# A fused attention-like and mixture-of-experts layer on one core: splitting two more products, folding dt into z's, and moving the router one loop pass later

## The reference, cut to what matters

```python
x = x + layernorm(attn(layernorm(x)))      # stage "p" makes q and h, stage "a" the rest
x = x + layernorm(ffn(layernorm(x)))       # stage "f"
# attn (a state-space mixer):
q = rope(x @ W_in[:256].T)                 # only q of qkv is used; it is also the residual
h = rmsnorm(q, norm_pre_w)
z, xBC, dt = split(h @ W_zxbcdt.T)         # 512, 768 and 8 columns
dt = softplus(dt + dt_bias); xBC = silu(conv4(xBC))
y = scan(x_ssm, dt, A, B, C) + D * x_ssm   # by chunks: decays exp(cumsum), a state between chunks
out = rmsnorm(y * silu(z), norm_gated_w) @ W_out.T + q
# ffn: a shared expert of 512 hidden and 16 routed ones of 64, the best 4 (of 2 groups) by token
c = route(sigmoid(x @ router_w.T) + correction_bias)
y = silu(x @ Wg) * (x @ Wu) [* c for the routed] @ Wd
```

## Time and profile before

| what | value |
|---|---|
| three runs | 3399.42, 3401.08, 5217.82 us (median 3401.08) |
| the profiled execution | 3397.91 us, span 3396.1 us |
| TensorE busy | 3259.8 us, 96% of the span, 18624 products |
| VectorE, GpSimd, ScalarE busy | 2450.5, 2159.6, 1830.1 us |
| mean granted TensorE clock | 0.987 of full speed |
| DMA | 210.40 MB, 62 GB/s on average |

### The profile page before, as it was taken

How to read it: one execution, slowest core, us unless ns; L and a number is a source line. 1 busy time by engine, 2 the same in 40 slices (tenths; PEclk the granted TensorE clock), 3 DMA queues, 4 the chain that set the end, 5 groups by cost and what they waited for, 6 DMA issues and landing times. The chain is left out here.

```text
span 3396.1 us, 58363 instructions
## 1 busy us (share of the span) xinstructions
PE 3259.8 (96%) x18624; PEld 2744.5 (81%) x18624; DVE 2450.5 (72%) x4881; ACT 1830.1 (54%) x3247; POOL 2159.6 (64%) x2247
## 2 busy tenths in 40 slices
PE   4799999999999999999999999999999999999997
PEld 3588888888888888888888888888888888888886
DVE  3677777777777777777777777777777777777772
ACT  3455555555555555555555555555555555555552
POOL 1476666776666776666776666766666766666764
PEclk8799999999999999999999999999999999999998
DMA  3022212112212112212122211122211122211121
GB/s 103 31 64 70 70 46 70 56 62 69 69 44 73 58 62 69 69 44 67 57 69 69 69 44 63 62 69 69 69 44 58 61 74 69 69 44 56 62 69 44
DMA packets 126236, 210.40 MB, mean 62 GB/s; under 512 B 18432, under 2 KB 71168, under 8 KB 126208
## 3 DMA queue, kind: packets, MB, share of 16 engines
q1 hardware_dynamic: 126208, 210.06, 18.8%
HBM read 174.87 MB, written 18.35 MB: 57 GB/s over the span
## 5 line engine op out<-in xcount | busy, mean ns | idle before, releaser
L524 POOL TENSOR_TENSOR hidL<-hid,hidH 128x512 fp32r<-128x512 f32 x384 | 492.8, 1283 | 670.3 <-ACT hidH L746 670.3
L951 DVE SCALAR_TENSOR_TENSOR xc<-apb,cw,xc 128x511 f32<-128x511 f32 (+2 forms) x576 | 430.7, 748 | 93.5 <-ACT xc L661 72.5
L519 POOL TENSOR_TENSOR hid<-hid,cb 128x512 f32<-128x512 f32 x256 | 412.7, 1612 | 75.9 <-POOL hidL L524 40.9
L1412 PE MATMUL acc<-WDH,hidH 128*128 128x256 f32 x1536 | 456.5, 297 | 4.4 <-POOLq L526 4.2
L1064 DVE TENSOR_TENSOR hid<-hid,fpb 128x512 f32<-128x512 f32 x384 | 263.6, 687 | 249.6 <-PE fpb L1240 205.2
L1412 PE MATMUL acc<-WDL,hidH 128*128 128x256 f32 x1536 | 433.0, 282 | 0.0
L1412 PE MATMUL acc<-WDH,hidL 128*128 128x256 f32 x1536 | 432.2, 281 | 0.0
L746 ACT CAST hidH<-hid 128x512 fp32r<-128x512 f32 x384 | 236.9, 617 | 333.1 <-POOL hid L519 321.9
L1240 PE MATMUL fpb<-fTh,GH 128*128 128x512 f32 x768 | 335.0, 436 | 6.5 <-ACTq L738 6.5
L1240 PE MATMUL fpb<-fTh,UH 128*128 128x512 f32 x768 | 326.8, 426 | 0.5 <-DVEq L867 0.5
L1412 PEld LDWEIGHTS acc<-WDH,hidH 128*128 128x128 f32 x1536 | 290.4, 189 | 30.0 <-POOLq L526 22.9
(11 more groups left out here) (185 smaller groups left out, 8427.0 us busy)
## 6 DMA issues: line engine op xcount, KB each, us to landing
seg<-acs_row SPq DMA_DIRECT2D x128, 512.0 KB, 5.1
cb<-c_row SPq DMA_DIRECT2D x512, 128.0 KB, 2.9
xsP<-in_x SPq DMA_DIRECT2D x32, 512.0 KB, 6.0
xs<-in_x SPq DMA_DIRECT2D x32, 512.0 KB, 5.3
x<-tmp SPq DMA_DIRECT2D x32, 512.0 KB, 2.9
out<-x SPq DMA_DIRECT2D x32, 512.0 KB, 2.9
ZL_loaded<-in_wzx_t SPq DMA_DIRECT2D x2, 640.0 KB, 5.4
GL_loaded<-in_wg_t SPq DMA_DIRECT2D x2, 512.0 KB, 6.6
```

Source lines behind the costliest of these rows:

```text
L519: G.tensor_tensor(hid[:, j % 2, :], hid[:, j % 2, :], cb[:, r % 2, :], ALU.mult).then_inc(sem["routed_ready"], 1)
L524: own.do(G.tensor_tensor(hidL[:, j % 2, :], hid[:, j % 2, :], hidH[:, j % 2, :].bitcast(fp32), ALU.subtract))
L951: ins = V.scalar_tensor_tensor(xc[:, b, s:], src[:, 0:T - s], cw[:, b, TAPS - 1 - s:TAPS - s], xc[:, b, s:], ALU.mult, ALU.add)
L1412: ins = nc.tensor.matmul(dst, l[:, w, tk], r[:, j, :], start=j == 0 and t % 2 == 0 and n == 0, stop=j == HB - 1 and n == 2, skip_group_che ...
```

## The change

- `WQ` and `WO` are kept as high and low parts (split at the start like the other weights); x's transposes (`xTh`, `xTl`, half a sequence each) and y's (`yTh`, `yTl`) too, and q's and the output's products are three `float32r` ones each.
- dt's eight columns stand behind the first half of z's; z is made in eight products of 264 or 256 columns (`za0`..`zb3`) instead of four of 512, and `project_dt` is gone.
- `exp_seg` takes the token's cumulated sum as the exponent's bias, in eight instructions of 128 columns, and `decay_exponents` is gone; `mask` waits for the DMA itself.
- q is copied by a DMA from `qrot` to `tmp`, which now shares memory with blocks 0 and 1 of `xc` (`xs` with 2 and 3); `mixed_out` adds in place. `norm_mixed` on ScalarE is gone: `add_x` multiplies by the norm's factor and adds x, and the norm's shift, a number per token, is left out of x1 there and added to the final norm's shift (`held`).
- x1 is stored into the output itself by `save_x1`, and GpSimd issues a DMA that adds the final normed result to it in DRAM (`accum_op`); `final_sum` and `store` are gone.
- The router's transposes and logits move from stage a to stage f, that is to the next pass, and the last two `down`s with the final norm to a new stage g, one pass later still. The loop now has 29 passes, after one with p, a and f, and there is one more pass at the end with g alone.
- All five lists are written in another order.

```diff
+            def save_x1(i):
                 sp.wait_ge(sem["x1_ready"], 1)
+                sp.dma_start(out[i].rearrange("(t p) d -> p t d", p=P), tmp).then_inc(sem["x1_stored"], 16)
+                sp.wait_ge(sem["x1_stored"], 16)
+                sp.sem_inc(sem["tmp_free"], 1)
+                sp.sem_inc(sem["x1_in_place"], 1)
+            def keep_q():
+                sp.wait_ge(sem["q_whole"], 1)
+                sp.wait_ge(sem["xc_read"], 1)
+                sp.dma_start(tmp, qrot[:]).then_inc(sem["q_kept"], 16)
...
+            def iteration(i, p, a, f, g):
+                if f: save_x1(i - 1)
+                if a: decay_store(); decay_rows(0); decay_rows(1)
+                if f: combine_store(); combine_rows(0)
+                if p: load_next(i + 1)
                 if f: combine_rows(1)
+                if a: decay_rows(2); decay_rows(3)
+                if f: combine_rows(2)
+                if a: keep_q()
+                if f: combine_rows(3)
+                if a: load_x(i)
+                if f: combine_rows(4); combine_rows(5); combine_rows(6); combine_rows(7)
                 if p: settle_p()
                 if a: settle_a()
...
+                G.tensor_scalar(fnm[:], fmv[:, :, 0], -1.0, 0.0, ALU.mult, ALU.add)
+                own.do(G.tensor_scalar(fve[:], fmv[:, :, 1], 1.0, EPS, ALU.mult, ALU.add))
+                own.do(G.tensor_tensor(frstd[:], fve[:], mhalf[:], ALU.pow))
+                own.do(G.tensor_tensor(fnm[:], fnm[:], frstd[:], ALU.mult))
+                own.do(G.tensor_tensor(fnm[:], fnm[:], held[:], ALU.add))
+                pool.sem_inc(sem["frstd_ready"], 1)
+            def hold_shift():
+                own.do(G.tensor_scalar(held[:], shift[:], 1.0, 0.0, ALU.mult, ALU.add))
+            def add_result(i):
                 pool.wait_ge(sem["normalised"], 1)
+                pool.wait_ge(sem["x1_in_place"], 1)
+                G.dma_start(out[i].rearrange("(t p) d -> p t d", p=P), xn[:], accum_op=ALU.add
+                            ).then_inc(s_stored, 16)
+            def result_stored():
+                pool.wait_ge(s_stored, 16)
+                G.inc_swdge_sem([s_stored], [16], mode="sub")
+                pool.sem_inc(sem["xn_free"], 1)
...
+            def iteration(i, p, a, f, g):
+                if g: norm_out()
+                if f: rest(0)
+                if g: add_result(i - 2)
+                if f: rest(1); rest(2)
                 if a: mask(0)
+                if f: hold_shift()
+                if a: mask(1)
+                if g: result_stored()
+                if a: decayed(0); decayed(1)
+                if f: rest(3); combine(4)
+                if a: gated(0)
...
+                if a: norm_mixed(1); norm_x1(0)
                 if f: combine(10)
                 if a: norm_x1(1)
+                if f: combine(11); rest(10); rest(11)
...
+                for h in range(HS):
+                    ins = A.activation(seg[:, c % 2, h, :], seg[:, c % 2, h, :], ACT.Exp,
+                                       bias=acs[:, 0, c * HS + h:c * HS + h + 1])
...
+            def iteration(p, a, f, g, w=False):
                 for names in freed.values():
                     names.clear()
                 if w: silu_table()
+                if a: conv_first(4); silu_z(0, 0); silu_z(1, 0)
+                if f: f_high(0); f_high(1)
+                if a: conv_first(5); conv_silu(4); silu_z(2, 0); conv_silu(5); exp_table(); softplus()
+                if a: conv_first(0); silu_table(); silu_z(3, 0)
                 if f: gate(0)
+                if a: conv_first(1); conv_silu(0)
+                if f: score_tanh()
+                if a: conv_first(2)
                 if f: round_hidden(0)
+                if a: conv_silu(1)
                 if f: gate(1)
+                if a: silu_z(0, 1); conv_silu(2)
                 if f: gate(2)
+                if g: final_norm()
+                if a: conv_first(3)
+                if f: round_hidden(1)
+                if a: silu_z(1, 1)
+                if f: round_hidden(2)
...
+                if a: evac_y(3); square_y(3)
                 if f: round_hidden(9)
+                if p: square_q(1)
+                if f: gate(10)
+                if p: h_high(0); h_high(1)
+                if f: gate(11)
                 if a: norm_x1(0)
                 if f: round_hidden(10)
+                if a: norm_x1(1)
                 if f: round_hidden(11)
...
+            def x_low(s):
+                dve.wait_ge(sem["xh_ready"], s + 1)
+                free("p", f"xT{s}", V.tensor_tensor(xTl[:], by_half(bank(f"xT{s}")), xTh[:].bitcast(fp32), ALU.subtract))
...
+            def dt_bias_add(c):
+                filled(dve, "DVE", f"za{c}")
+                ins = V.tensor_tensor(dr[:, c, :], bank(f"za{c}")[:, DI // 2:DI // 2 + HS], dtb[:], ALU.add)
+                if c < NT - 1:
+                    ins.then_inc(sem["dt_read"], 1)
+                else:
+                    own.do(ins)
+                    dve.sem_inc(sem["dt_read"], 1)
+                    V.scalar_tensor_tensor(na[:], dr[:], -1.0, dr[:], ALU.mult, ALU.min).then_inc(sem["na_ready"], 1)
...
+                dve.wait_ge(sem["mixed_stats"], s + 1)
                 if s == 0:
                     dve.wait_ge(sem["x_loaded"], 16)
-                own.do(V.tensor_tensor(tmp[:, pair(s), :], tmp[:, pair(s), :], xs[:, pair(s), :], ALU.add))
+                for t in ts:
+                    ins = V.scalar_tensor_tensor(tmp[:, t, :], tmp[:, t, :], rstd[:, t:t + 1], xs[:, t, :],
+                                                 ALU.mult, ALU.add)
+                own.do(ins)
...
+            def iteration(p, a, f, g, w=False):
+                for names in freed.values():
+                    names.clear()
+                if a: dt_bias_add(0); dt_bias_add(1); conv(4)
+                if f: f_low(0)
+                if a: dt_bias_add(2)
+                if f: f_low(1)
+                if a: conv(5)
+                if f: route_logits()
+                if a: dt_bias_add(3)
+                if g: final_moments()
+                if a: dt_finish(); conv(0)
+                if f: up(0)
+                if a: conv(1); conv(2)
+                if f: route_scores()
+                if a: evac_acs()
+                if f: up(1); route_groups(); up(2)
+                if a: conv(3)
+                if f: route_experts(); up(3)
+                if a: times_dt(0); times_dt(1); decay_CB(0)
                 if f: up(4)
+                if a: new_state(0); chunk_y(0)
                 if f: up(5)
+                if a: state_part(1); decay_CB(1)
+                if a: new_state(1); times_dt(2); chunk_y(1)
+                if p: moments_px()
                 if f: up(6)
+                if a: state_part(2); decay_CB(2); y_low(0); new_state(2)
+                if a: chunk_y(2); times_dt(3); decay_CB(3)
+                if p: x_low(0)
+                if a: y_low(1)
                 if f: up(7)
+                if p: rope(0)
+                if a: mixed_out(0)
+                if a: state_part(3)
                 if f: up(8)
+                if a: chunk_y(3); y_low(2)
+                if p: x_low(1)
+                if a: add_x(0)
                 if f: up(9)
+                if a: y_low(3)
+                if p: rope(1); norm_q(0)
                 if a: mixed_out(1)
                 if f: up(10)
+                if p: norm_q(1); h_low(0)
                 if a: add_x(1)
+                if p: h_low(1)
                 if f: up(11)
...
-                    tk = slice((2 * s + t) * P, (2 * s + t + 1) * P)
-                    for k in range(KD):
-                        ins = nc.tensor.matmul(b[:, t * D:(t + 1) * D], xT[:, k, tk], WQ[:, k, :],
-                                               start=k == 0, stop=k == KD - 1)
+                    tk = slice(t * P, (t + 1) * P)
+                    ins = split_mm(b[:, t * D:(t + 1) * D], [(xTh[:, k, tk], xTl[:, k, tk], WQH[:, k, :], WQL[:, k, :])
+                                                             for k in range(KD)])
...
+            def project_z(c, n):
+                name, tk = f"z{'ab'[n]}{c}", slice(c * P, (c + 1) * P)
+                cs = slice(DI // 2 + HS, ZC) if n else slice(0, DI // 2 + HS)
+                b = slot(name)
+                if c == 0 and n == 0:
+                    pe.wait_ge(s_hT, 2)
+                    pe.sem_inc(s_hT, -2)
+                fill(name, split_mm(b[:, 0:cs.stop - cs.start], [(hTh[:, k, tk], hTl[:, k, tk], ZH[:, k, cs], ZL[:, k, cs])
+                                                                 for k in range(KD)],
+                                    sem["hT_read"] if c == NT - 1 and n == 1 else None))
...
-                for j in range(NB):
-                    ins = nc.tensor.matmul(b[:, (t % 2) * D:(t % 2 + 1) * D], yT[:, t % 2, j, :], WO[:, j, :],
-                                           start=j == 0, stop=j == NB - 1)
```

(54 more changed lines are left out.)

610 lines of the change are left out of this document (256 added, 354 removed).

## The result

The changed kernel takes **3217.73 us** (median of 4 runs, 3214.39 to 3220.89), the kernel before 3401.12 beside it: ratio **0.946, 95% interval 0.9445 to 0.9478**. The profiled execution took 3218.34 us (span 3216.4).

The account below looks back on a forecast made before the run. TensorE's list of products plus its waits bounds thirty equal passes of 102.2 us. Products -3.5 and waits -0.8 a pass give -129; with the ends, -123 from 3397.9, so 3277 us; range 3230 to 3335.

Parts of the forecast that it names:

- these two: TensorE's waits before h's second transposes (0.86 us) and before xc4 (0.36), said to hold nearly all 1.35 us idle.
- the ends: Outside the thirty passes: last pass with stage two -3, first 0, head +2, last sequence's end +6, accumulating DMA +1.
- rival 2: Waits vanish altogether and TensorE runs on rows alone: pass of 97.3 us, total time 3249 us; chance 0.10.
- The products' term: TensorE's work per pass: q and output -1.86, dt's narrow block -1.76, z's halves +0.12, together -3.5 us.
- The same products on TensorE: 0: Moving router, its transposes, the last two downs and final norm one pass later: no change in TensorE's work, only waits.
- rival 1: Waits stay or grow under the tighter list, 1.35 to 2.5 us a pass: total time 3300 to 3335 us; chance 0.26.
- 0.1 to 0.4 us: Wait of z's first product for cast and low part of h's second transposes, with only up(11) between.
- up to 0.8 more: Wait at the third z half, whose bank ScalarE frees late after its settling: 6.0 us against TensorE's 5.2.
- The first one is bound by its chain: 0: The first pass with the second stage in it was to gain nothing, being bound by its chain.
- Rival 3: GpSimd's accumulating DMA lands after its cover before decayed(0) and state(0), some 13 us: slower; chance with its like 0.06.
- second price: The accumulating DMA's issue holds GpSimd, delaying rest(1) behind it; said to be covered for some 5 us.
- ScalarE's eight exponentials at nothing: exp_seg's eight instructions for one add 5.8 us to ScalarE a pass, costed at nothing since it stays below TensorE.

Follow-up runs that it names:

- experiment 6: Against the kernel before: VectorE's first rotation in the first full pass moved ahead of the fifth and sixth weight low-part subtractions; first distance 106.30 us, 106.5 before.

## Why the prediction was wrong, step by step

**The step that failed: "The idle of the pass is 102.17 - 100.82 = 1.35 us, nearly all in these two", and the 0.8 us taken from it.** Shown: the idle is 0.16 us short at each wait, so "these two" are 1.54 us between starts and not 1.22, and taking at them gave 0.52 and 0.44. There were two more, of 0.29 and 0.17, shown as 0.13 and 0.01. Of these 2.0 us one wait of 0.21 is left, where I kept 0.55. All in all the waits fell by about 2.4 us; the remaining 0.6 lies in steps of 0.1 or 0.2 us at the borders of blocks, most of them in the blocks around those waits, and no run separates their causes. The pass came out 1.5 us below the forecast: 1.6 to 1.7 more of waits, 0.2 less of products. Over thirty passes that is 44 of the 59 us missed; the ends below are 12, and the rest is what the profiled executions differ from the medians. Even rival 2, with the waits gone altogether, took 1.35 and so ended at 3249.

**The products' term was right**: -3.5 forecast, -3.3 by the starts, +1.83 and +1.74 when put back. By the four passes that the Trainium skill (FP8 and Floating Point Precision, TensorE Precision Notes) states for true FP32, three reduced products would come to 0.75 of a full one, an estimate. The blocks give 1.42/1.73 = 0.82 again, as before, and putting full products back cost 0.305 us a block where 0.75 asks for 0.43. The row was the better price.

**Right for a reason that the forecast didn't have.** It wrote for the router and the last `down`s an iteration later "The same products on TensorE: 0" and saw in it only a new wait of up to 0.8 us. In the old list 1.3 us of narrow products were worth nothing (102.25) and came back as a wait, which is rival 1's mechanism. They count in full only after the end-of-pass chain and GpSimd's sum are relieved (100.15). The changed kernel does both: moments and normalisation of the last `down`s stand inside the next pass, off the settling, and the sum is a transfer. The wait of 0.29 us ahead of x1's second transposes is gone too where these stand one pass later. This shows that such relief is needed in the old list; the move alone was not tried in either kernel, so its share of the 2.4 us isn't separated.

**"0.1 to 0.4 us" for z's first product** was 0.21. **"up to 0.8 more" at za2** didn't come.

**The ends: forecast +6, measured -6.3**, 12 us of the miss. Which of +2, +6 and +1 failed isn't separated, and the scatter is as large. "The first one is bound by its chain: 0" can't be kept in that form: its first distance fell by 9.0 us. But 5.6 of these only come from where the marking matmul stands in the pass: behind seven gate and up blocks and a `down` before, and behind four now (4 x 1.41). The wait of 10.9 us in the first pass of the kernel before ends with GpSimd's list, where small operations stand stretched beside VectorE's weight subtractions (experiment 6); no run takes that collision away, so what it costs isn't measured.

**Rival 3** didn't come because the landing took 6.0 us; its cover of "some 13 us" agrees with the trace (13.3) and wasn't tested. Its second price has too large a cover ("some 5 us"; some 3), and it costs 2.5 us a pass when the wait stands right behind the issue. **ScalarE's eight exponentials at nothing**: shown.

## What to carry to other kernels

Read the bounding engine's waits between starts, not as idle: short ones hide under the modelled tail of the instruction before. Before booking a saved instruction, ask which chain ends just behind it: in the old list the same 1.3 us were worth 0 and, with 1.6 us of ScalarE and a GpSimd sum out of the way, all of it. When an engine is made to wait, follow also the buffers it has yet to read, since their next writer waits too.

## What the runs showed of the hardware

- An accumulating store of 512 KB from GpSimd landed in 6.0 us, a plain one from the same place in 3.5, SyncE's in 3.0.
- A 1024-column sum on GpSimd stretches whichever small VectorE operation runs beside it, from about 0.2 to 2.3 or 2.4 us, and which one it hits depends on 1 us of timing. The other way round, beside VectorE's subtraction of 1536 columns an operation of two columns on GpSimd took 1.6 us for 0.19.
- The end of a pass costs ScalarE 1.78 us between its last and its next instruction, and a chain that crosses it pays for it.
